# Fewer groups looked up ahead of the first step of a graph-convolution kernel, and two per step until the lead is reached

## The chip, the cores and the metric

One core of one Trainium2 chip runs the kernel as one launch. The metric is the device time in microseconds (us), median of the runs shown. PE is TensorE (PEld its weight loads), DVE is VectorE, ACT is ScalarE, POOL is GpSimd, SP is SyncE. "Span" is the time between first and last instruction of the profiled execution.

## The reference, cut to what matters

100,000 nodes with 128 features, 25,000 edges with a type out of 50, sorted by `dst`; `src` is random.

```python
h = maximum(layernorm(x), 0)                       # eps 1e-5
deg = segment_sum(ones, row)                       # row = src, col = dst
deg_inv = where(deg > 0, rsqrt(maximum(deg, 1)), 0)
norm = deg_inv[row] * deg_inv[col]
hj_b = comps[edge_type][:, :, None] * h[col][:, None, :]
msg = einsum('ebd,bdf->ef', hj_b, bases) * alpha[edge_type] * norm[:, None]
return x + segment_sum(msg, row)                   # 4 bases of 128 x 128
```

## The kernel before, in words

The 25,000 edges are 196 tiles of 128; four tiles are a group, so there are 49 groups. `x` is copied to the output by SP in 50 DMAs of 2,000 rows (`copy`, L295), at most two in flight. The edges' messages are then added onto the copy by indirect DMAs with an add, so POOL waits for all 50 copies before its first scatter (L365 to L367). Every engine has its own hand-written program, and semaphores alone tie them together. Within an engine, instructions run in the order written. The stages:

- **Histogram (degrees).** For each tile DVE writes one-hot rows of `src` (`hots`, L441 and L442) and PE multiplies them into four banks (L696), so that after 196 tiles the banks hold all degrees. After each 14 tiles comes a "type part": DVE's `type_hots(i)` (L434), PE's `turn_types(i)` (L688) and ACT's `keep_coef(i)` (L590). There are 14 parts; `turn_types(i)` waits until `keep_coef(i - 2)` has run, and DVE's `type_hots(i)` until `turn_types(i - 2)` has. POOL meanwhile gathers the rows `x[dst]` of 80 tiles (L356), and ACT takes their means and squares group by group (`stats(g)`, L575 to L583). ACT's program puts `keep_coef(i)` and the load of a later type row (`load_types`, L253) between the `stats`; `types_before(g)` says how many parts are kept before `stats(g)`.
- **Look-up.** To fetch the degrees of a tile's two ends, DVE writes one-hots of a whole group (`turned_hots(g)`, L458, four instructions, two buffers), PE multiplies them with the table of degrees (`look(t)`, eight matmuls at L710 into one of two banks), and DVE picks the value of each edge (`pick(t)`, two instructions at L464). `look(t)` waits for `pick(t - 2)`, `turned_hots(g)` for the looks of group g - 2, and the row of edges it reads is loaded by `load_edge_row(g)` (L260), which waits for `turned_hots(g - 4)`. Before, 8 groups (`LEAD`) are looked up ahead of step 0.
- **Norms.** For 7 groups at a time DVE computes degree products and variance (`norms_in`, L475 to L480), ACT a root (L595), DVE the coefficients (`norms_out`, L487 to L492).
- **49 steps**, one per group. PE turns the group's `h` (L720) and multiplies each tile by the four bases (`multiply(t)`, L729, waits for `message(t - 4)`); ACT takes the first base's part (`first(t)`, L620), DVE adds the three others (`combine`, L499), pair by pair of tiles. In the same step the group 8 ahead is looked up, one tile after each `multiply`. DVE also compares source ids within tiles (`same_src`, L518). From step 3 on, PE sums messages of equal source (`add_same`, L737 and L739), up to five tiles a step, ACT copies each sum into one of six buffers (`keep_sum`, L630), and POOL scatters it (L377). ACT runs `stats` of further groups at the end of a step: `stats_until(step)` is 21 + 2 (step + 1) groups, as far as gathered. POOL has gathered 112 tiles before its first scatter, and mixes the other 84 in, seven for ten scatters.

In ACT's program before the steps, five `load_edge_row` calls (groups 4 to 8) stand ahead of `stats(16)` to `stats(20)` (L639 to L642), and the last `keep_coef` calls stand behind some of them.

## Time and profile before

| what | value |
|---|---|
| median of 3 runs | 777.32 us (770.5 to 780.03) |
| the profiled execution | 778.24 us |
| its span | 776.5 us |
| mean granted TensorE clock | 0.919 |
| busy: PE, DVE, ACT, POOL | 74%, 77%, 47%, 69% |

The profiled execution lies 0.9 us above the median, and 1.7 us of it lie outside the span. Busy shares are means over stages with different limits, so the time is read stage by stage: the histogram until about 152 us, the look-ups until about 210 us, the steps until about 750 us, and the last scatters.

### The profile page before, as it was taken

Reading aid. Unit: us, or ns where it says so; the run is one execution under the profiler, and the core shown is the slowest. Engines: PE = TensorE matmul, PEld = TensorE weight load, DVE = VectorE, ACT = ScalarE, POOL = GpSimd, SP = SyncE. Lnnn points to the kernel's source line nnn. Section 1 sums busy time; section 2 is a strip of 40 time slices with the busy share of each in tenths; the row PEclk is TensorE's granted clock in tenths of the full one; section 3 lists DMA queues with packets and bytes.
Section 4 is the critical chain, followed back from the end, with each engine's and each line's share of the span. In section 5 each row is a group of like instructions: output and inputs, shape, how many; then the busy total and the mean of one; then the engine's idle time right before and its main releaser. Section 6 shows DMA issues by size and latency. Waiting matters only on the chain.

```text
span 776.5 us, 13645 instructions
## 1 busy us (share of the span) xinstructions
PE 575.3 (74%) x3922; PEld 408.1 (53%) x3922; DVE 596.3 (77%) x2613; ACT 368.7 (47%) x1493; POOL 538.5 (69%) x404
## 2 busy tenths in 40 slices
PE   1966795455776986687786977886898878898861
PEld 0744464444644754455554655654666656665530
DVE  4974795666777988677696979996989899998740
ACT  0155633153267554464455555565466634445630
POOL 1886687646500787877788887888888666667785
PEclk9996998778788999999899999998999999999995
DMA  3989999989811354444444545534444454534433
GB/s 114 341 308 339 338 351 314 354 283 337 308 33 55 73 95 76 82 93 78 96 78 87 93 63 117 94 56 94 93 93 84 82 93 81 100 58 55 59 34 28
DMA packets 56527, 108.89 MB, mean 140 GB/s; under 512 B 9291, under 2 KB 48216, under 8 KB 55636
## 3 DMA queue, kind: packets, MB, share of 16 engines
q0 software_dynamic: 34496, 25.72, 24.6%
q1 hardware_dynamic: 5372, 55.14, 19.6%
q10 hardware_dynamic: 16584, 27.16, 11.4%
q8 instruction: 32, 0.52, 0.3%
q14 instruction: 43, 0.35, 0.1%
HBM read 94.89 MB, written 64.61 MB: 205 GB/s over the span
## 4 chain that ended last, share of the span: by engine, by line
DVE 28%; PE 22%; DMA 14%; issue 12%; ACT 11%; POOL 8%; another core or an unknown queue 2%; SPq 1%; ACTq 0%; POOLq 0%; DVEq 0%
DMA out_dram<-acc,scatter_idx 9%; PE pst L710 7%; PE pst L696 6%; DVE masked L464 6%; POOL out_dram L377 5%; PE pst L729 5%; DVE part_sum L499 5%; DVE turned_hot L458 4%; DMA rows<-in_x_dram,dst_i 4%; POOL rows L356 3%; ACT scratch L583 3%; DVE rows L441 3%; ACT scratch L575 3%; DVE same L518 3%; DVE rows L499 2%
## 5 line engine op out<-in xcount | busy, mean ns | idle before, releaser
L377 POOL DMA_INDIRECT out_dram<-acc,scatter_idx x196 | 313.4, 1599 | 132.2 <-ACT acc L630 62.0
L356 POOL DMA_INDIRECT rows<-in_x_dram,dst_i x196 | 223.0, 1138 | 98.8 <-issue 40.9
L710 PE MATMUL pst<-table_bits,turned_hot 128*128 128x198 f16 x1568 | 181.4, 263 | 59.3 <-DVE masked L464 50.5
L729 PE MATMUL pst<-bases_sb,h_turned 128*128 128x512 f32 x392 | 212.6, 625 | 0.0
L710 PEld LDWEIGHTS pst<-table_bits,turned_hot 128*128 128x128 f16 x1568 | 145.9, 104 | 86.4 <-issue 52.8
L499 DVE SCALAR_TENSOR_TENSOR part_sum<-pst,coef,part_sum 128x128 f32<-128x128 f32 x392 | 115.8, 344 | 89.6 <-ACT part_sum L620 88.2
L737 PEld LDWEIGHTS pst<-rows,same 128*128 128x128 f32 x392 | 71.6, 197 | 177.7 <-issue 154.3
L464 DVE SCALAR_TENSOR_TENSOR masked<-iota_h,lo,pst 128x198 f32<-128x198 f16 x392 | 141.6, 415 | 16.9 <-PE pst L710 14.9
L620 ACT ACTIVATE part_sum<-pst,coef 128x128 f32<-128x128 f32 x196 | 71.2, 363 | 139.6 <-PE pst L729 102.9
L737 PE MATMUL pst<-rows,same 128*128 128x128 f32 x392 | 83.4, 296 | 66.1 <-ACT acc L630 62.1
L575 ACT ACTIVATE scratch<-rows 128x128 f32<-128x128 f32 x196 | 57.8, 297 | 135.8 <-DMA rows<-in_x_dram,dst_i 100.4
L696 PE MATMUL pst<-rows 128*128 128x198 f16 x784 | 94.3, 270 | 26.6 <-DVE rows L442 15.7
L630 ACT ACTIVATE acc<-pst,sum_scale 128x128 f32<-128x128 f32 x196 | 71.6, 365 | 77.2 <-DMA out_dram<-acc,scatter_idx 58.7
L441 DVE TENSOR_SCALAR rows<-iota_h,src_hi 128x512 f16<-128x512 f16 x196 | 68.7, 350 | 34.8 <-PE pst L696 19.0
L696 PEld LDWEIGHTS pst<-rows 128*128 128x128 f16 x784 | 67.0, 106 | 51.3 <-DVE rows L442 32.4
L518 DVE SCALAR_TENSOR_TENSOR same<-src_row,src_f,later 128x256 f32<-128x256 int32 x196 | 87.3, 478 | 0.0
L458 DVE TENSOR_SCALAR turned_hot<-edge_row,chunk_id 128x1024 f16<-128x1024 f16 x196 | 85.6, 499 | 0.0
L739 PE MATMUL pst<-acc,same 128*128 128x128 f32 x390 | 78.3, 284 | 0.0
L583 ACT ACTIVATE scratch<-rows,less_mean 128x128 f32<-128x128 f32 x196 | 76.2, 390 | 2.5 <-ACT less_mean L579 1.0
L729 PEld LDWEIGHTS pst<-bases_sb,h_turned 128*128 128x128 f32 x392 | 62.0, 199 | 0.1
L739 PEld LDWEIGHTS pst<-acc,same 128*128 128x128 f32 x390 | 62.0, 200 | 0.0
L604 ACT ACTIVATE h<-rows,less_mean 128x128 f32<-128x128 f32 x196 | 61.9, 390 | 0.0
(71 smaller groups left out, 414.5 us busy)
## 6 DMA issues: line engine op xcount, KB each, us to landing
out_dram<-in_x_dram SPq DMA_DIRECT2D x50, 1000.0 KB
src_row<-src_rows ACTq DMA_DIRECT2D x25, 512.0 KB
edge_row<-edge_rows ACTq DMA_DIRECT2D x45, 256.0 KB
rows<-in_x_dram,dst_i POOLq DMA_INDIRECT x196
out_dram<-acc,scatter_idx POOLq DMA_INDIRECT x196
rows<-edge_rows ACTq DMA_DIRECT2D x10, 175.0 KB
edge_row<-edge_rows SPq DMA_DIRECT2D x4, 256.0 KB
src_row<-src_rows SPq DMA_DIRECT2D x2, 512.0 KB
```

The lines of the kernel that those rows point to most:

```text
L356: pool.indirect_dma_start(row(t), None, x, bass.IndirectOffsetOnAxis(ap=dst_i[:, t:t + 1], axis=0)) \
L377: pool.indirect_dma_start(out, bass.IndirectOffsetOnAxis(ap=scatter_idx[:, t:t + 1], axis=0), acc[:, t % ACC_RING, :], None, compute_op=AL ...
L458: last = dve.tensor_scalar(turned_hot[:, g % 2, c, :], hi, chunk_id[:, c:c + 1], None, ALU.is_equal)
L464: last = dve.scalar_tensor_tensor(out=masked[:, 2 * (t % 2) + k, :], in0=iota_h[:, 0:LO], scalar=lo[:, k, t:t + 1], in1=pst[:, LOOK + t % ...
L499: dve.scalar_tensor_tensor(out=to, in0=pst[:, PRODUCT + t % 4, term * D:(term + 1) * D], scalar=coef[:, t, term:term + 1], in1=part_sum[:, ...
L518: dve.scalar_tensor_tensor(out=same[:, t % SAME_RING, 0:w], in0=src_row[:, b, j * P:j * P + w], scalar=src_f[:, t:t + 1], in1=later[:, 0:w ...
L583: last = act.activation(scratch[:, 1, j, :], row(t), ACT.Square, bias=less_mean[:, t:t + 1], accum_out=squares[:, t:t + 1])
L696: last = pe.matmul(pst[:, HIST + c, 0:LO], hots[:, b, c * P:(c + 1) * P], hots[:, b, CHUNKS * P:], start=(t == 0), stop=(t == TILES - 1))
L710: last = pe.matmul(pst[:, LOOK + t % 2, k * LO:(k + 1) * LO], turned_hot[:, g % 2, c, k * W + j * P:k * W + (j + 1) * P], table[:, c * LO: ...
L729: pe.matmul(pst[:, PRODUCT + t % 4, :], h_turned[:, g % 2, j, :], bases_sb[:].rearrange("d b f -> d (b f)"), start=True, stop=True).then_i ...
L737: last = pe.matmul(pst[:, SUMS, 0:D], same[:, t % SAME_RING, 0:P], row(t), start=True, stop=(t == 0))
L739: last = pe.matmul(pst[:, SUMS, 0:D], same[:, (t - 1) % SAME_RING, P:2 * P], acc[:, (t - 1) % ACC_RING, :], start=False, stop=True)
```

## The change

Three groups (`FIRST_LOOK`) instead of eight are looked up ahead of step 0. `look_until(step)` is min(49, step + 9, 3 + 2 (step + 1)): steps 0 to 4 look up two groups each (3 and 4, 5 and 6, and so on to 11 and 12), and from step 5 on one group each, 8 ahead, as before. In a step with two groups PE makes two looks after each `multiply`, and DVE picks four tiles after each pair. The norms come in batches that end at groups 3, 7, 14, 21 and so on. ACT makes 18 instead of 21 `stats` before the steps, keeps the type parts earlier among them (four for five `stats` instead of seven for ten), and loads the edge rows of groups 4 and on at the start of the steps, two for a step while two groups are looked up. POOL makes gathers 80 to 87 paced by the looks and 88 to 111 paced by the products of steps 0 to 2.

```diff
+    FIRST_LOOK = 3
+    NORM_AT = (0, 3, *range(NORM_GROUPS, GROUPS + 1, NORM_GROUPS))
...
+    def look_until(step):
+        return min(GROUPS, step + LEAD + 1, FIRST_LOOK + 2 * (step + 1))
+
+    def looks_at(step, j):
+        a, b = (GROUP * look_until(s) for s in (step - 1, step))
+        return list(range(a + (b - a) * j // GROUP, a + (b - a) * (j + 1) // GROUP))
...
-    HIST_GATHERS, FIRST_GATHERS = 80, 112
+    HIST_GATHERS, LOOK_GATHERS, FIRST_GATHERS = 80, 88, 112
...
-    STATS_BEFORE = 21
+    STATS_BEFORE = 18
 
     def types_before(g):
-        return min(TYPE_PARTS, max(0, (7 * g + 6) // 10))
+        return min(TYPE_PARTS, max(0, (4 * g + 3) // 5))
...
-                elif HIST_GATHERS <= t < FIRST_GATHERS:
-                    pool.wait_ge(look_ps, (t - HIST_GATHERS + 1) * LEAD * GROUP // (FIRST_GATHERS - HIST_GATHERS))
+                elif HIST_GATHERS <= t < LOOK_GATHERS:
+                    pool.wait_ge(look_ps, (t - HIST_GATHERS + 1) * FIRST_LOOK * GROUP // (LOOK_GATHERS - HIST_GATHERS))
+                elif LOOK_GATHERS <= t < FIRST_GATHERS:
+                    pool.wait_ge(product_ready, (t - LOOK_GATHERS) // 2 + 1)
...
             for k in range(GROUPS):
-                ahead = k + LEAD
                 for pair in range(0, GROUP, 2):
                     combine(range(k * GROUP + pair, k * GROUP + pair + 2))
-                    if ahead < GROUPS:
-                        for j in (pair, pair + 1):
-                            pick(ahead * GROUP + j)
+                    for j in (pair, pair + 1):
+                        for t in looks_at(k, j):
+                            pick(t)
+                            looked = t + 1
                     if pair == 0:
-                        if ahead + 1 < GROUPS:
-                            turned_hots(ahead + 1)
+                        while hots_done < min(GROUPS, looked // GROUP + 2, look_until(k) + 1):
+                            turned_hots(hots_done)
+                            hots_done += 1
...
-                after = STATS_BEFORE - 1 - g
-                if after < LEAD + 1 - EDGE_RING:
-                    load_edge_row(act, LEAD - after)
                 stats(g)
-            batch = 2
+            batch, edge, rooted = 2, EDGE_RING, 1
             root(0)
             relu(0)
...
             for k in range(GROUPS):
-                if k + LEAD + 1 < GROUPS:
-                    load_edge_row(act, k + LEAD + 1)
+                while edge < min(GROUPS, look_until(k) + 1):
+                    load_edge_row(act, edge)
+                    edge += 1
...
             pe.wait_ge(table_ready, CHUNKS)
-            for t in range(LEAD * GROUP):
+            for t in range(FIRST_LOOK * GROUP):
                 look(t)
```

The line numbers of the changed kernel are higher by 10 to 18; the operations are the same. In ACT's program at the end of the `stats` before the steps, the kernel before has (L590 is `keep_coef`, L260 `load_edge_row`, L575 to L583 `stats`; the first row here is the square of `stats(15)`):

```order
L583 ACTIVATE scratch,squares<-rows,less_mean 128x128 x4
L260 DMA edge_row<-edge_rows 128x2x512
L575 ACTIVATE scratch,row_sum<-rows 128x128 x4
L579 ACTIVATE less_mean<-row_sum 128x4
L583 ACTIVATE scratch,squares<-rows,less_mean 128x128 x4
L590 ACTIVATE coef_parts<-pst 128x168
L260 DMA edge_row<-edge_rows 128x2x512
L575 ACTIVATE scratch,row_sum<-rows 128x128 x4
L579 ACTIVATE less_mean<-row_sum 128x4
L583 ACTIVATE scratch,squares<-rows,less_mean 128x128 x4
L590 ACTIVATE coef_parts<-pst 128x168
L260 DMA edge_row<-edge_rows 128x2x512
L575 ACTIVATE scratch,row_sum<-rows 128x128 x4
L579 ACTIVATE less_mean<-row_sum 128x4
```

and the changed kernel, at the same place (L605 is `keep_coef`, L590 to L598 are `stats`; from `stats(15)` to the root):

```order
L598 ACTIVATE scratch,squares<-rows,less_mean 128x128 x4
L605 ACTIVATE coef_parts<-pst 128x168
L590 ACTIVATE scratch,row_sum<-rows 128x128 x4
L594 ACTIVATE less_mean<-row_sum 128x4
L598 ACTIVATE scratch,squares<-rows,less_mean 128x128 x4
L605 ACTIVATE coef_parts<-pst 128x168
L590 ACTIVATE scratch,row_sum<-rows 128x128 x4
L594 ACTIVATE less_mean<-row_sum 128x4
L598 ACTIVATE scratch,squares<-rows,less_mean 128x128 x4
L611 ACT_TABLE_LOAD
L611 ACTIVATE norm_root<-norm_in 128x12
```

No edge row is loaded among the `stats` any more, and the last `keep_coef` stands ahead of `stats(17)` instead of `stats(20)`.

On DVE, between the last look-ups ahead of the steps and the end of step 0, the kernel before has (L458 `turned_hots`, L464 `pick`, L499 `combine`, L518 `same_src`, L487 to L492 `norms_out`):

```order
L458 TENSOR_SCALAR turned_hot<-edge_row,chunk_id 128x1024 x4
L464 SCALAR_TENSOR_TENSOR masked,picked<-iota_h,lo,pst 128x198 x8
L487 TENSOR_TENSOR coef_sum<-coef_parts 128x112
L488 TENSOR_TENSOR coef_sum<-coef_sum,coef_parts 128x112
L490 RECIPROCAL norm<-norm_root 128x28
L491 TENSOR_TENSOR norm<-norm,has_degree 128x28
L492 TENSOR_TENSOR coef<-coef_sum,norm 128x112
L499 SCALAR_TENSOR_TENSOR part_sum<-pst,coef,part_sum 128x128 x4
L499 SCALAR_TENSOR_TENSOR rows<-pst,coef,part_sum 128x128 x2
L464 SCALAR_TENSOR_TENSOR masked,picked<-iota_h,lo,pst 128x198 x4
L458 TENSOR_SCALAR turned_hot<-edge_row,chunk_id 128x1024 x4
L518 SCALAR_TENSOR_TENSOR same,copies<-src_row,src_f,later 128x256
```

and the changed kernel (L470 `turned_hots`, L476 `pick`, L513 `combine`, L532 `same_src`, L488 to L493 `norms_in`, L501 to L506 `norms_out`):

```order
L476 SCALAR_TENSOR_TENSOR masked,picked<-iota_h,lo,pst 128x198 x8
L488 TENSOR_SCALAR variance<-squares 128x12
L493 TENSOR_TENSOR norm_in<-norm_in,variance 128x12
L501 TENSOR_TENSOR coef_sum<-coef_parts 128x48
L506 TENSOR_TENSOR coef<-coef_sum,norm 128x48
L513 SCALAR_TENSOR_TENSOR part_sum<-pst,coef,part_sum 128x128 x4
L513 SCALAR_TENSOR_TENSOR rows<-pst,coef,part_sum 128x128 x2
L476 SCALAR_TENSOR_TENSOR masked,picked<-iota_h,lo,pst 128x198 x8
L470 TENSOR_SCALAR turned_hot<-edge_row,chunk_id 128x1024 x8
L532 SCALAR_TENSOR_TENSOR same,copies<-src_row,src_f,later 128x256
L513 SCALAR_TENSOR_TENSOR part_sum<-pst,coef,part_sum 128x128 x4
L476 SCALAR_TENSOR_TENSOR masked,picked<-iota_h,lo,pst 128x198 x8
```

`norms_in` now stands straight ahead of `norms_out`, with no `turned_hots` and no picks between them, and a step has eight picks' instructions and two groups' one-hots where it had four and one.

On PE the first two tiles of step 0 read before (L720 turns `h`, L729 is `multiply`, L710 `look`):

```order
L720 MATMUL pst<-ident,h 128x128 x8
L729 MATMUL pst<-bases_sb,h_turned 128x512
L710 MATMUL pst<-table_bits,turned_hot 128x198 x8
L729 MATMUL pst<-bases_sb,h_turned 128x512
L710 MATMUL pst<-table_bits,turned_hot 128x198 x8
```

and now (L733 `turn`, L742 `multiply`, L723 `look`):

```order
L733 MATMUL pst<-ident,h 128x128 x8
L742 MATMUL pst<-bases_sb,h_turned 128x512
L723 MATMUL pst<-table_bits,turned_hot 128x198 x16
L742 MATMUL pst<-bases_sb,h_turned 128x512
L723 MATMUL pst<-table_bits,turned_hot 128x198 x16
```

Each `multiply` has 16 matmuls of look-ups behind it instead of 8.

## Rows read from the trace of the kernel before

**Rows 1.** Stretches of 25 us: length, busy us (instructions) by engine, PE clock, DMA share, GB/s

```profile
core 0: us, PE busy (x) PEld busy (x) DVE busy (x) ACT busy (x) POOL busy (x), PEclk, DMA share, GB/s
...
450.00:475.00 25.00, 19.40 (x122) 13.87 (x121) 20.50 (x92) 11.74 (x44) 19.58 (x15) 0.93 0.46 79
...
650.00:675.00 25.00, 22.72 (x157) 16.68 (x156) 23.71 (x105) 12.00 (x36) 17.14 (x11) 1.00 0.42 70
```

**Rows 2.** The same over 2 us after the copies (same columns)

```profile
217.00:219.00 2.00, 2.00 (x18) 1.43 (x16) 2.00 (x7) 0.55 (x3) 0.00 (x0) 1.00 0.00 0
```

**Rows 3.** Timeline of POOL: start, us, engine, line, what; [idle before it, and its releaser]

```profile
253.32 1.63 POOL L377 DMA_INDIRECT out_dram<-acc,scatter_idx  x1 [42.63 <-ACT acc L630]
...
284.07 1.56 POOL L377 DMA_INDIRECT out_dram<-acc,scatter_idx  x1 [0.30 <-issue]
```

**Rows 4.** Timeline of PE in the histogram, at a type part (L688); columns as in rows 3

```profile
127.11 0.52 PE L688 MATMUL pst<-comps_split,rows 50*128 50x12 bf16 x14 [5.48 <-ACT coef_parts L590]
```

**Rows 5.** Timeline of ACT: keep_coef (L590) after stats(0), and the wait at an edge row load

```profile
34.14 0.29 ACT L590 ACTIVATE coef_parts<-pst 128x168 f32<-128x168 f32 x1
...
156.32 0.31 ACT L575 ACTIVATE scratch<-rows 128x128 f32<-128x128 f32 x1 [16.94 <-DVE turned_hot L458]
```

**Rows 6.** Groups by line, 20 to 54 us: busy us, mean ns | idle before, releasers

```profile
L356 POOL DMA_INDIRECT rows<-in_x_dram,dst_i x18 | 28.8, 1601 | 10.1 <-PE pst L696 9.2 <-issue 0.9
L441 DVE TENSOR_SCALAR rows<-iota_h,src_hi 128x512 f16<-128x512 f16 x70 | 24.2, 346 | 0.0
```

**Rows 7.** Groups by line, 160 to 210 us (the look-ups)

```profile
L356 POOL DMA_INDIRECT rows<-in_x_dram,dst_i x32 | 31.8, 994 | 24.1 <-PE pst L710 15.6 <-issue 7.3 <-remote 1.1
...
L688 PE MATMUL pst<-comps_split,rows 50*128 50x12 bf16 x14 | 0.5, 169 | 8.0 <-ACT coef_parts L590 8.0
```

**Rows 8.** Timeline of all engines: first look, then the changeover to the steps

```profile
160.31 7.19 PE L710 MATMUL pst<-table_bits,turned_hot 128*128 128x198 f16 x48
...
203.23 0.18 DVE L475 TENSOR_SCALAR variance<-squares 128x28 f32<-128x28 f32 x1
...
204.45 2.43 ACT L604 ACTIVATE h<-rows,less_mean 128x128 f32<-128x128 f32 x8
...
209.50 0.42 DVE L464 SCALAR_TENSOR_TENSOR masked<-iota_h,lo,pst 128x198 f32<-128x198 f16 x1 [0.55 <-PE pst L710]
...
211.50 1.02 PE L729 MATMUL pst<-bases_sb,h_turned 128*128 128x512 f32 x2
...
214.14 0.37 ACT L620 ACTIVATE part_sum<-pst,coef 128x128 f32<-128x128 f32 x1 [0.66 <-PE pst L729]
```

**Rows 9.** Groups by line, 211 to 300 us: what a step is made of

```profile
L710 PE MATMUL pst<-table_bits,turned_hot 128*128 128x198 f16 x232 | 28.2, 270 | 9.5 <-DVE masked L464 9.2 <-issue 0.2
...
L464 DVE SCALAR_TENSOR_TENSOR masked<-iota_h,lo,pst 128x198 f32<-128x198 f16 x56 | 20.1, 416 | 0.0
L499 DVE SCALAR_TENSOR_TENSOR part_sum<-pst,coef,part_sum 128x128 f32<-128x128 f32 x56 | 16.7, 345 | 15.9 <-ACT part_sum L620 15.9
...
L458 DVE TENSOR_SCALAR turned_hot<-edge_row,chunk_id 128x1024 f16<-128x1024 f16 x28 | 11.8, 486 | 0.0
```

**Rows 10.** Timeline of ACT in step 2 and at the start of step 3

```profile
237.87 0.34 ACT L620 ACTIVATE part_sum<-pst,coef 128x128 f32<-128x128 f32 x1
...
244.38 0.37 ACT L620 ACTIVATE part_sum<-pst,coef 128x128 f32<-128x128 f32 x1 [4.01 <-PE pst L729]
...
250.83 0.35 ACT L620 ACTIVATE part_sum<-pst,coef 128x128 f32<-128x128 f32 x1
251.08 0.35 ACT L630 ACTIVATE acc<-pst,sum_scale 128x128 f32<-128x128 f32 x1
```

**Rows 11.** The chain that ended last, in order of time (start, us, what)

```profile
65.42 4.65 another core or an unknown queue
```

**Rows 12.** Timeline: ACT issues the load of type row 4; DVE uses it

```profile
32.62 0.56 ACTq L253 DMA_DIRECT2D rows<-edge_rows  x1
...
50.88 0.68 DVE L434 TENSOR_SCALAR rows<-rows,chunk_id 50x1792 bf16<-50x1792 f16 x1
```

75 lines of the change are left out of this document (39 added, 36 removed).

## The prediction

> **What bounds the kernel now.** I read the stretches of 25 us first, then POOL's timeline, then PE's and ACT's timelines of the histogram and of the changeover to the steps. In the stretch from 450 us POOL is busy 19.58 of 25 us with 15 instructions, and each has 0.30 us of issue ahead of it: 24.1 of 25 us [rows 1, 3]. So POOL's scatters and gathers set the pace of the middle of the kernel. Late in the kernel, when the gathers are done, DVE is the fuller engine (from 650 us 23.71 of 25 us, POOL 17.14 with 11 scatters) [rows 1]. The first scatter starts at 253.32 us, after POOL has idled 42.63 us for ACT's first sum [rows 3]. The copies that it must also wait for are over by 217 us, when DMA traffic is zero [rows 2]. So the end of the kernel follows the first scatter: whatever brings it forward comes through to the end, as long as POOL stays fed afterwards. At most 36 us can be won there (253.3 to about 217).
>
> What lies ahead of the first scatter is a chain of four pieces: the histogram up to the first look at 160.31 us, the look-ups up to the first `multiply` at 211.50 us, and steps 0 to 2 with the start of step 3 up to the scatter, 41.8 us [rows 3, 8]. The change touches every piece.
>
> **First look (removed waits).** PE could not begin to look at 160.31 us sooner because its last type part waited 8.0 us for a `keep_coef` [rows 7], and ACT, which makes it, stood 16.94 us at the load of edge row 4, until DVE's first one-hots were written [rows 5]. The edge rows leave this place, so this wait goes. That alone lets looks start when the one-hots are there, at 156.3 at the latest: 4 us.
>
> The earlier `keep_coef` calls do more. Within the histogram PE waits for them too, 5.48 us at one part [rows 4], because they stand behind `stats` that wait for gathers. The last part on which PE waits needs `keep_coef(11)`, and that now stands behind `stats(14)` instead of `stats(16)`. So the look-ups can start when 15 groups are gathered and treated. `stats(0)` is done at 34.14 us [rows 5]. While DVE writes one-hots without a pause a gather takes 1.60 us plus 0.30 us of issue, 7.6 us for a group [rows 3, 6], and 14 more groups end at 34.1 + 14 x 7.6 = 140.7 us. At the pace of the look-up stage (0.99 + 0.30, 5.2 us a group [rows 7]) they end at 107 us, and then the histogram is its own limit: 70 tiles in 34 us are 0.49 us a tile [rows 6], so 196 tiles from just before 20 us end by about 113 us and looks start at some 117 us. Against this stand pauses in which nothing that the trace names is waited for, the longest of them 4.65 us [rows 11]; I see no reason for them to go. Bounds: 117 and 156.3 us. I take 138 us, near the slow pace, a little less because PE still has pauses in which gathers run quickly. That is 22 us earlier than now (bounds 4 and 43).
>
> On that pace the Trainium skill (SBUF — State Buffer, section "SBUF: two separate sides") says that a VectorE instruction in a two-port mode locks GpSimd out for its whole length, so that indirect DMAs issued there wait to have their descriptors written. The two means, 1.60 us beside the one-hots and 0.99 us beside the look-ups, agree with it. By this rule a histogram with fewer pauses gathers more slowly, which speaks against the change: its own limit would be 140.7 us, and without the rule 117 us.
>
> **Look-ups and changeover.** Eight groups take 160.31 to 209.50 us, 6.15 us a group; three take 18.4 us. Before, the norms (begun at 203.23 us) and ACT's eight ReLU instructions (204.45 us, 2.43 us long) ran beside the look-ups of group 7, and `multiply(0)` came 2.0 us after the last pick's start [rows 8]. Now nothing covers them. After the last look: two picks 0.8 us, norms and root 1.2 us (203.23 to 204.45), ReLUs 2.4 us, ACT's copy of the turned group and the semaphores 0.9 us: 5.3 us. So `multiply(0)` follows the first look by 23.7 us instead of 51.2 us, a gain of 27 us (bounds 24 and 29, by 3 us more or 2 us less of exposed work). `multiply(0)` would start at 162 us.
>
> **Steps 0 to 2 (added work).** In step 2 ACT goes from `first(8)` at 237.87 to `first(11)` at 244.38 (6.5 us), does two `stats` (6.45 us) and starts `first(12)` at 250.83: 12.96 us a step [rows 10]. The first 6.5 us are a chain through the engines, and the second group's look-ups lie right in it. By busy time over count in [rows 9], a `combine` of a pair is 6 x 0.298 = 1.8 us, a pick 2 x 0.359 = 0.72 us, a look 8 x 0.122 = 0.97 us, one group's one-hots 4 x 0.42 = 1.7 us. From `first(b)`, 0.75 us into the step: `combine` 1.8; then PE's third and fourth look, each waiting for a pick, with DVE's picks 3.4; the one-hots of the second group, which PE has not had before, 1.7; two looks 1.9; `multiply` 1.1; semaphores 0.9. Sum 11.6 us to `first(d)`. With `stats` 6.45 us and the return to `first` that makes 18.2 us instead of 12.96 us: 5.3 us more a step. The picks and one-hots behind `first(d)` fit beside the two `stats`. Step 0 has one look more ahead of its second product (1 us), and the four-group norms between steps 1 and 2 hold ACT's root by about a microsecond. Together 3 x 5.3 + 2, and 2 for uneven starts: 20 us. Bounds: 9 us (one look more a tile hidden, 3 us a step) and 35 us (10 us of work for each further group wholly in line with DVE's present step). The first scatter then comes at 162 + 41.8 + 20 = 224 us, behind the end of the copies, so the floor of 217 us does not act.
>
> **Steps 3 and 4 (POOL fed more slowly).** Before, the eleventh scatter starts 30.75 us after the first [rows 3], with POOL never idle. The eleventh sum is made in step 5. Two double steps of 18.2 us, with three `add_same` in the chain of each, put it about 40 us after the first (an `add_same` is four matmuls in the records, and at a look's 0.122 us each [rows 9] about 0.5 us: 36.4 + 6 x 0.5 = 39.4 us). POOL waits for the difference, 9 us (bounds 0 and 17). From step 5 on the program is the same as before, and POOL, which is the limit there, cannot make it up. This is what I would expect a reader to overlook: the first scatter gains 29 us, the end only 20.
>
> **Sum.** 22 + 27 - 20 - 9 = 20 us. From the profiled 778.2 us that is 758 us; the profiled execution lies 0.9 us above the median, which changes nothing at this accuracy. So the five groups that leave the lead-in are paid back nearly whole in the double steps (27 against 29), and what stays is the earlier start of the look-ups.
>
> **Rivals.**
> - *The histogram does not shorten.* The looks then start at 156.3 us, 4 us earlier, and the other terms give 4 + 27 - 29 = 2: 776 us. For it: the unnamed pauses, and the slow gathers, which a denser histogram makes slower. Against it: PE's measured waits for `keep_coef` [rows 4, 7].
> - *The double steps hide their looks.* DVE idles 15.9 us at `combine` between 211 and 300 us [rows 9]. If that takes up half of the work, the steps cost 10 us and POOL stays fed: 22 + 27 - 10 = 39, cut by the end of the copies to 36: 742 us.
> - *Edge rows land late, and it is slower.* Two edge rows a step are now issued just ahead of the step that uses them, some 8 us before DVE needs the first, while the copies still fill the DMA engines (steps 0 to 2 lie between 162 and 217 us). The nearest row is a type row issued at 32.62 us and used at 50.88 us without a wait [rows 12], so a broadcast under the copies takes at most 18 us. If it takes all of that, each of three steps waits 10 us more: 20 - 30 = -10, 788 us. It decides once the wait exceeds 6 to 7 us a step. Against it: the 18 us are only an upper bound, since the row may have lain there long before it was used.
>
> **How the numbers follow.** The forecast has a chance of 0.5, with a range of its own from 748 to 768 us; the unshortened histogram 0.2; the hidden looks 0.2; the late edge rows 0.07; anything else 0.03. Two per cent, about what a measurement of this kernel can tell from no change, is 762 us and 793 us. Of the forecast's half, 0.33 lies below 762 us. With the hidden looks that is 0.53 for faster; 0.43 for within two per cent, with the first and most of the third rival; 0.04 for slower. The range from 740 to 780 us leaves out the late edge rows and the ends of the others.
>
> **What would show it.** Right: PE's first look near 138 us with no `keep_coef` wait of 8 us ahead of it; `multiply(0)` about 24 us later; steps 0 to 4 of some 18 us each with DVE waiting for `first(d)`; the first scatter near 224 us; POOL idle between scatters 6 and 11 and without gaps after them. Wrong: a first look later than 150 us, double steps under 15 us, a first scatter held by the last copy, or waits of DVE's one-hots for `edge_row`.

## The result: slower by one per cent, where 2.6% faster was forecast

| | us |
|---|---|
| this kernel, median of 12 runs | 780.93 (773.57 to 785.49) |
| kernel before, median of 12 runs on the same chip | 773.75 (768.83 to 783.61) |
| ratio, 95% interval | 1.0099 (1.0063 to 1.0134) |
| predicted | 758.0, range 740 to 780 |

By the 2% bound this is no change; by its interval it is a small, real loss. The profiled execution took 785.49 us (span 783.6), 4.6 us above its median; it is the slowest of the twelve and counts as a slow run, which the ratio leaves out, while e13 below profiles the same kernel in a fast run. Differences of a few microseconds between two profiles are left to the ratios.

**Profile after.** Its page begins as follows; the 40 slices are 19.6 us each.

```profile
span 783.6 us, 13659 instructions
...
PE 583.6 (74%) x3922; PEld 414.5 (53%) x3922; DVE 597.8 (76%) x2624; ACT 371.0 (47%) x1494; POOL 538.4 (69%) x404
...
PEclk9996898967888889999899999998999999999995
```

No engine gained or lost noticeable work, so the loss is waiting. The two stretches that answer to [rows 1] (same columns) still show POOL as the fuller part of the middle, and DVE late:

```profile
450.00:475.00 25.00, 20.77 (x129) 14.88 (x129) 20.78 (x94) 11.97 (x43) 20.73 (x15) 0.93 0.50 105
650.00:675.00 25.00, 21.95 (x152) 16.29 (x151) 23.79 (x109) 10.92 (x31) 16.19 (x11) 1.00 0.49 81
```

Milestones of the two profiled executions, read from the timelines of PE and POOL, beside what was forecast:

| start of, us | before | forecast | after | after less before |
|---|---|---|---|---|
| first look | 160.31 | 138 | 145.58 | -14.7 |
| `multiply(0)` | 211.50 | 162 | 173.46 | -38.0 |
| first scatter | 253.32 | 224 | 242.02 | -11.3 |
| eleventh scatter | 284.07 | 264 | 286.82 | +2.8 |
| last scatter | 768.6 | | 775.7 | +7.1 |

The lead-in did shorten by 38 us. All of it is gone again by the eleventh scatter. POOL's timeline after (columns as in [rows 3]) shows the second half of the loss:

```profile
242.02 1.63 POOL L389 DMA_INDIRECT out_dram<-acc,scatter_idx  x1 [8.72 <-issue]
...
257.02 1.78 POOL L389 DMA_INDIRECT out_dram<-acc,scatter_idx  x1 [2.82 <-ACT acc L646]
263.65 1.57 POOL L389 DMA_INDIRECT out_dram<-acc,scatter_idx  x1 [3.53 <-ACT acc L646]
...
272.02 1.60 POOL L389 DMA_INDIRECT out_dram<-acc,scatter_idx  x1 [3.59 <-ACT acc L646]
...
286.82 1.56 POOL L389 DMA_INDIRECT out_dram<-acc,scatter_idx  x1 [5.10 <-ACT acc L646]
290.00 1.81 POOL L389 DMA_INDIRECT out_dram<-acc,scatter_idx  x1 [0.30 <-issue]
```

Before, POOL had 0.30 us of issue ahead of the eleventh scatter [rows 3]; now it waits for ACT's sum again and again up to it, and behind it about as rarely as before. From the first to the eleventh scatter it is 44.8 us instead of 30.75 us (46.9 us in e13).

The first half is in steps 0 to 2, which start at 173.46, 195.19 and 217.36 us, with step 3 at 237.40 us: 21.7, 22.2 and 20.0 us each, where 18.2 us was forecast and 12.96 us was the step of before [rows 10]. The chain that ended last runs through them. Here is a part of it (start, us, what) from the end of step 0 to step 4:

```profile
189.65 1.17 ACT scratch L590 x8
...
194.16 0.43 ACT scratch L598 x2
194.60 13.96 DMA edge_row<-edge_rows
209.07 1.72 DVE turned_hot L470 x4
210.79 0.81 DVE same L532 x4
211.60 1.04 DVE part_sum L513 x4
212.63 0.52 DVE rows L513 x2
213.15 0.69 DVE masked L476 x4
213.89 2.82 PE pst L723 x16
216.71 0.85 PE pst L733 x4
217.56 1.63 PE pst L742 x2
...
233.93 2.82 PE pst L723 x16
236.75 0.85 PE pst L733 x4
237.60 1.71 PE pst L742 x2
...
256.21 1.17 ACT scratch L590 x8
257.64 1.65 ACT scratch L598 x8
259.29 1.18 ACT scratch L590 x8
260.73 0.79 ACT scratch L598 x3
```

Three things are to be read here. The load of an edge row stood in ACT's program behind the two `stats` of step 0, took 13.96 us to land, and DVE's one-hots (L470) waited 3.56 us for it. From there to `multiply(12)`, at the start of step 3, the chain goes through one-hots, `combine` (L513), picks (L476), looks (L723), `turn` (L733) and `multiply` (L742), and ACT is not in it. From step 3 on ACT's `stats` (L590, L598) stand in it themselves.

ACT's and PE's timelines over the end of step 2 say the same from the side of the wait:

```profile
230.64 0.37 ACT L636 ACTIVATE part_sum<-pst,coef 128x128 f32<-128x128 f32 x1 [3.77 <-PE pst L742]
...
239.40 0.37 ACT L636 ACTIVATE part_sum<-pst,coef 128x128 f32<-128x128 f32 x1 [2.23 <-issue]
```

```profile
228.15 1.56 PE L723 MATMUL pst<-table_bits,turned_hot 128*128 128x198 f16 x16 [1.69 <-DVE turned_hot L470]
...
233.93 2.82 PE L723 MATMUL pst<-table_bits,turned_hot 128*128 128x198 f16 x16 [3.33 <-DVE masked L476]
```

From `first(11)` to `first(12)` it is 8.76 us, where it was 6.45 us for the two `stats` before [rows 10]; the same way in steps 0 and 1 takes 7.11 and 11.18 us, where it was 6.44 us before. In step 2 ACT finishes them and then idles 2.23 us, because `multiply(12)` stands on PE behind the last looks of step 2. Those looks are also slow. After an idle of 3.33 us sixteen of their matmuls take 2.82 us instead of 1.56 us, and the granted clock of that stretch is 0.50, the 1.2 GHz level (stretches of 2 us, columns as in [rows 1]):

```profile
228.00:230.00 2.00, 1.85 (x17) 1.62 (x18) 1.97 (x7) 0.00 (x0) 1.49 (x2) 1.00 0.11 33
234.00:236.00 2.00, 2.00 (x13) 1.83 (x14) 1.08 (x7) 1.94 (x13) 0.00 (x0) 0.50 0.11 33
```

### The profile page after: what moved, and what is told of

It is laid out like the page before. It is cut to its first block, busy times and chain, and to the rows that moved or that the text cites. A ratio compares the mean times of both kernels' runs of the same rounds, so it can differ in the third digit from the quotient of the medians.

```text
span 783.6 us, 13659 instructions
## 1 busy us (share of the span) xinstructions
PE 583.6 (74%) x3922; PEld 414.5 (53%) x3922; DVE 597.8 (76%) x2624; ACT 371.0 (47%) x1494; POOL 538.4 (69%) x404
## 3 DMA queue, kind: packets, MB, share of 16 engines
q10 hardware_dynamic: 16584, 27.16, 11.6%
## 4 chain that ended last, share of the span: by engine, by line
DVE 24%; PE 19%; issue 17%; DMA 16%; POOL 15%; ACT 7%; another core or an unknown queue 1%; SPq 1%; ACTq 0%; POOLq 0%; DVEq 0%
DMA out_dram<-acc,scatter_idx 12%; POOL out_dram L389 10%; PE pst L723 6%; PE pst L709 5%; POOL rows L368 5%; DVE masked L476 4%; PE pst L742 4%; DVE turned_hot L470 4%; DVE rows L453 4%; DVE part_sum L513 3%; DVE rows L454 3%; ACT scratch L598 2%; DMA edge_row<-edge_rows 2%; DVE rows L513 2%; DVE same L532 2%
## 5 line engine op out<-in xcount | busy, mean ns | idle before, releaser
L723 PE MATMUL pst<-table_bits,turned_hot 128*128 128x198 f16 x1568 | 181.5, 265 | 80.9 <-DVE masked L476 61.6
L742 PE MATMUL pst<-bases_sb,h_turned 128*128 128x512 f32 x392 | 218.1, 640 | 0.0
L723 PEld LDWEIGHTS pst<-table_bits,turned_hot 128*128 128x128 f16 x1568 | 147.2, 105 | 108.3 <-issue 52.5
L513 DVE SCALAR_TENSOR_TENSOR part_sum<-pst,coef,part_sum 128x128 f32<-128x128 f32 x392 | 115.8, 344 | 98.6 <-ACT part_sum L636 92.3
L750 PEld LDWEIGHTS pst<-rows,same 128*128 128x128 f32 x392 | 74.4, 203 | 168.1 <-issue 147.2
L476 DVE SCALAR_TENSOR_TENSOR masked<-iota_h,lo,pst 128x198 f32<-128x198 f16 x392 | 141.8, 416 | 18.9 <-PE pst L723 11.6
L590 ACT ACTIVATE scratch<-rows 128x128 f32<-128x128 f32 x196 | 57.7, 297 | 94.0 <-DMA rows<-in_x_dram,dst_i 87.4
L453 DVE TENSOR_SCALAR rows<-iota_h,src_hi 128x512 f16<-128x512 f16 x196 | 68.4, 349 | 26.8 <-PE pst L709 15.5
L470 DVE TENSOR_SCALAR turned_hot<-edge_row,chunk_id 128x1024 f16<-128x1024 f16 x196 | 85.5, 500 | 3.6 <-DMA edge_row<-edge_rows 3.6
L532 DVE SCALAR_TENSOR_TENSOR same<-src_row,src_f,later 128x256 f32<-128x256 int32 x196 | 87.3, 478 | 0.4 <-issue 0.4
L752 PE MATMUL pst<-acc,same 128*128 128x128 f32 x390 | 79.9, 289 | 0.0
L598 ACT ACTIVATE scratch<-rows,less_mean 128x128 f32<-128x128 f32 x196 | 76.2, 390 | 2.0 <-ACT less_mean L594 0.5
L752 PEld LDWEIGHTS pst<-acc,same 128*128 128x128 f32 x390 | 63.7, 205 | 0.0
L742 PEld LDWEIGHTS pst<-bases_sb,h_turned 128*128 128x128 f32 x392 | 63.5, 204 | 0.2
```

The lines of the kernel that those rows point to most:

```text
L453: dve.tensor_scalar(hots[:, b, 0:CHUNKS * P], iota_h[:], src_hi[:, t:t + 1], None, ALU.is_equal)
L470: last = dve.tensor_scalar(turned_hot[:, g % 2, c, :], hi, chunk_id[:, c:c + 1], None, ALU.is_equal)
L476: last = dve.scalar_tensor_tensor(out=masked[:, 2 * (t % 2) + k, :], in0=iota_h[:, 0:LO], scalar=lo[:, k, t:t + 1], in1=pst[:, LOOK + t % ...
L513: dve.scalar_tensor_tensor(out=to, in0=pst[:, PRODUCT + t % 4, term * D:(term + 1) * D], scalar=coef[:, t, term:term + 1], in1=part_sum[:, ...
L532: dve.scalar_tensor_tensor(out=same[:, t % SAME_RING, 0:w], in0=src_row[:, b, j * P:j * P + w], scalar=src_f[:, t:t + 1], in1=later[:, 0:w ...
L723: last = pe.matmul(pst[:, LOOK + t % 2, k * LO:(k + 1) * LO], turned_hot[:, g % 2, c, k * W + j * P:k * W + (j + 1) * P], table[:, c * LO: ...
```

## The experiments

Every ratio is against the kernel before on the same chip. No run has a profile of the kernel before on the second group's chips; e10, which has its lead-in, stands in for it there. The changed kernel and e1 to e8 ran on chips on which it takes 774 to 775 us, the others on chips on which it takes 754 to 755 us, so only ratios are compared between the two groups, never times. "Milestones" are first look, `multiply(0)`, first scatter, eleventh scatter, from one profiled execution each.

### What the earlier type parts bring: e1 and e2

e1 is the kernel before with the new times of the `keep_coef` calls alone; e2 is the changed kernel with the old times and 21 groups of `stats` ahead of the steps.

```diff
# e1, on before
-        return min(TYPE_PARTS, max(0, (7 * g + 6) // 10))
+        return min(TYPE_PARTS, max(0, (4 * g + 3) // 5))
# e2, on after
-    STATS_BEFORE = 18
+    STATS_BEFORE = 21
-        return min(TYPE_PARTS, max(0, (4 * g + 3) // 5))
+        return min(TYPE_PARTS, max(0, (7 * g + 6) // 10))
```

> The kernel before with one thing of the change alone: keep_coef four parts for five stats (types_before) instead of seven for ten; eight groups are still looked up ahead of step 0, and the edge rows are still loaded among the stats. Theory 1 (in the change the histogram part gained and the double steps gave it back): the first look starts at about 145 us as in the changed kernel (145.58) instead of 160.31, everything behind it moves by the same amount, the first scatter comes at about 239 us, the time is 13 to 16 us shorter than before: ratio 0.980 to 0.984. Rival A (the earlier keep_coef is not what brought the first look forward, it was the removal of the edge rows from among the stats): the first look stays later than 155 us, ratio 0.995 to 1.00. Rival B (an earlier first scatter is lost again behind it, because something other than POOL's scatters sets the end): first look at 145 us, but ratio above 0.99.

> The changed kernel with the histogram part undone: keep_coef again seven parts for ten stats, 21 stats ahead of the steps; still no edge row loads among them, three groups ahead of step 0 and two a step. Theory 1: the first look goes back to about 156 us (10 us later than in the changed kernel), but steps 0 to 4 have three stats fewer between them, worth 3 x 3.2 us mostly in steps 3 and 4; time 0 to 8 us longer than the changed kernel, ratio to the kernel before 1.01 to 1.02. Rival A (the edge rows were what held the first look): first look stays near 146 us and the time falls by the stats saved, ratio to before about 1.00.

Measured: e1 0.998 (0.9945 to 1.0014), milestones 138.14, 204.17, 248.1, 277.47. e2 1.0034 (1.0004 to 1.0064), milestones 153.41, 177.27, 244.46, 282.54.

In e1 the first look comes 22 us earlier, just what the prediction's first term said, and yet `multiply(0)` only 7.3 us earlier: the look-ups now take 66.0 us instead of 51.2 us. DVE's waits (us in total, times, longest) give one reason, before and in e1:

```profile
DVE rows L441 <- remote: 15.5, 5, 4.7
```

```profile
DVE masked L464 <- remote: 18.1, 4, 10.6
```

"Remote" are the pauses of [rows 11], in which nothing that the trace names is waited for. Before, they fell into the histogram (L441); in e1 most of them fell into the look-ups (L464). But they are not the whole reason. e12 and e10, below, ran on a chip without such pauses and differ ahead of the steps by the early type parts alone: the first look comes 11.7 us earlier (130.69 instead of 142.38 us), and `multiply(0)` only 2.8 us (182.63 instead of 185.41 us). In e12's look-ups ACT waits 20.7 us for gathered rows (e10: 5.8 us) ahead of its `stats`, and the loads of the edge rows stand in its program behind them:

```profile
DVE turned_hot L460 <- DMA edge_row<-edge_rows: 6.3, 3, 3.7
```

So on that chip the look-ups that start earlier wait for edge rows, and these for the gathers (the row is from 130 to 183 us). e2 changes two things at once and does not price the early type parts: without them and with three more groups of `stats` ahead of the steps, the changed kernel is no worse, rather 0.65% better (intervals that just touch).

### What slows the double steps: e4, e3, e11, e8

```diff
# e4, on after (e8: the same on before, with the types of e1)
-        return min(STATS_BEFORE + 2 * (step + 1), ...)
+        return min(STATS_BEFORE + (step + 1), ...)
# e3, on after: edge rows 4 to 7 ahead of root(0); at the end of step k, ahead of the stats
+                while edge < min(GROUPS, look_until(k + 2) + 1):
+                    load_edge_row(act, edge)
+                    edge += 1
# e11, on after, ahead of the looks of j = 1 and 3 in steps 0 to 4; u = 4k + j + 1
+                        pe.wait_ge(message_ready, u - 3)
+                        for _ in range(10):
+                            pe.matmul(pst[:, PRODUCT + u % 4, 0:LO], iota_h[:, 0:P], iota_h[:, 0:LO],
+                                      start=True, stop=True)
```

The matmuls added in e11 keep PE busy and are never read.

> The changed kernel with one stats call at the end of a step instead of two (the total is the same, spread over more steps, in which ACT has room). Theory 1 (ACT's two stats stand in line with the doubled look-up chain): each of steps 0 to 4 gets 3.2 us shorter, the first scatter comes some 9 us earlier (233 us), POOL is fed 6 us better in steps 3 and 4, time 10 to 15 us shorter than the changed kernel, ratio to before 0.99 to 0.995. Rival D (the stats are beside DVE's picks of the second pair, so DVE's work takes their place): steps shorten by less than 1.5 us each, time within 5 us of the changed kernel.

> The changed kernel with each edge row loaded one step earlier: rows 4 to 7 ahead of ACT's first root, then the two of step k + 2 at the end of step k. Rival C (late edge rows make the double steps slow): DVE's wait for an edge row (3.56 us once, after a load that took 13.96 us to land) goes, the first scatter comes 4 us or more earlier than the 242.0 us of the changed kernel, and the time is 4 to 10 us shorter than the changed kernel's (ratio to before 0.995 to 1.004). Theory 1 (the looks, picks and one-hots in line are what cost): steps 0 to 4 still take 18 to 21 us each, the time is 0 to 4 us shorter.

> The changed kernel with ten extra matmuls (128x198, f16, result never read) on PE ahead of the second and fourth pair of looks in each of steps 0 to 4, where PE idles 2.6 us now and then runs the looks at half clock (16 matmuls in 2.82 us instead of 1.56). Theory 3 (the lower clock after these idles is what makes a double step 22 us instead of the 18 forecast): the looks behind them take 1.56 us, the way from the first multiply to the first scatter falls from 68.6 us by 5 us or more, time 5 to 8 us shorter than the changed kernel. Theory 1 without the clock: the way gets no shorter, or longer by up to 1.3 us per group of extra matmuls, time the same or up to 5 us longer.

> The kernel before (eight groups looked up ahead, single steps) with the early keep_coef and with one stats call per step instead of two. Theory 1 (two stats stand in line in every early step, also in single ones): steps 0 to 3 take 10 us instead of 13, the first scatter comes 7 to 9 us earlier than with the early keep_coef alone, time 764 to 768 us, ratio to before 0.985 to 0.991, shorter than both kernels. Rival: POOL is as late with one stats call because gathers then wait for stats: no gain over the early keep_coef alone (0.998).

| | ratio (95%) | `multiply(0)` to first scatter | first to eleventh |
|---|---|---|---|
| before | 1 | 41.8 | 30.75 |
| after | 1.0099 (1.0063 to 1.0134) | 68.6 | 44.8 |
| e4 | 0.9954 (0.9919 to 0.999) | 64.3 | 38.1 |
| e3 | 1.0076 (1.0038 to 1.0114) | 64.3 | 45.6 |
| e11 (after there: 69.5, 46.9) | 1.007 (1.0038 to 1.0102) | 69.3 | 42.7 |
| e8 | 0.9966 (0.9924 to 1.0007) | 37.3 | 30.15 |

One `stats` fewer per step is the largest single piece: 1.4% against the changed kernel, 11 us on the way to the eleventh scatter, of which 6.7 us lie behind the first scatter and only 4.3 us in steps 0 to 2. That fits the chain above, in which `stats` stand from step 3 on. Up to the eleventh scatter POOL's scatters wait 9.8 us for ACT's sums in e4, and 17.0 us in the changed kernel. In steps 0 to 2 of e4 the way from `first(d)`, the last `first` of a step, to the next step's first one still takes 9.97, 7.85 and 7.89 us, though one `stats` is only 3.2 us, and ACT idles 6.52, 4.40 and 4.44 us at its end:

```profile
196.22 0.37 ACT L636 ACTIVATE part_sum<-pst,coef 128x128 f32<-128x128 f32 x1 [6.52 <-PE pst L742]
```

So in these steps it is the work on DVE and PE behind `first(d)` that is waited for, not the `stats`.

The early edge rows (e3) take away the wait for the load (no such row in DVE's waits) and 4.3 us of steps 0 to 2, but the time only moves within its uncertainty (its profile is of its fastest run, 771.61 us; the median is 780.15 us). In e11 most looks of the double steps run at the 2.4 GHz level, and two groups of sixteen, behind longer idles, still do not:

```profile
170.39 2.82 PE L723 MATMUL pst<-table_bits,turned_hot 128*128 128x198 f16 x16 [6.03 <-DVE masked L476]
...
180.83 1.56 PE L723 MATMUL pst<-table_bits,turned_hot 128*128 128x198 f16 x16 [1.71 <-DVE masked L476]
```

The mean granted clock between `multiply(0)` and the first scatter is 0.91 instead of 0.75 in e13, and the way is as long as there, 69.3 us against 69.5 us. The time gains 0.3 to 0.5% against the changed kernel, with overlapping intervals. So the half clock is not shown to cost anything here; what the added matmuls themselves cost is not known apart. e8 shows the same cut of `stats` on the kernel before: the steps get shorter by 6.7 us against e1, and 3.3 us are left at the eleventh scatter. That would be 0.4% of the time, and the ratio moves by 0.14%, which its interval cannot tell from either.

### The copies, and the pauses: e5, e6, e7

e5 (on before) and e6 (on after) leave out 48 of the 50 copies from the input to the output, so most output rows lack their input part. e7 is the changed kernel with 100 copies of half the size.

```diff
# e5, e6
-            for i in range(1, COPIES):
-                copy(i)
+            copy(1)
-                sp.wait_ge(copied[b], 16 * (COPIES // COPY_RING))
+                sp.wait_ge(copied[b], 16)
# e7
-    COPIES = 50
+    COPIES = 100
```

> The kernel before, leaving out 48 of the 50 copies of x to the output (rows 4,000 and up are not copied), so that the lead-in has the DMA engines nearly to itself. If the copies are behind the unnamed pauses and the slow gathers: no pause of the unnamed kind is left, the first look comes at 115 to 130 us, the first multiply some 45 to 50 us later, the first scatter at 205 to 215 us, time 730 to 740 us. If the pauses are not due to the copies: they stay, and the first look is later than 140 us.

> The changed kernel with the same 48 copies left out. Theory 1 (the chain of doubled looks, and POOL fed late in steps 3 and 4, give back what the shorter look-up won, whatever the DMA load): the eleventh scatter comes within 5 us of that of the kernel before without copies, and the two times lie within 6 us of each other. Rival (theory 2: the change loses because its double steps 0 to 2 now lie under the copies, with late edge rows and pauses): without copies the changed kernel is at least 10 us shorter than the kernel before without copies, with double steps of 15 us or less.

> The changed kernel with 100 copies of 1,000 rows instead of 50 of 2,000, still two in flight, so that half as much stands queued in the DMA engines ahead of a gather, an edge row or an instruction fetch. Theory 2 (the queue of the copies is what delays the lead-in and steps 0 to 2): gathers land in about 5 us instead of 7.5, the edge row load that took 13.96 us takes less than 9, the pauses halve, time 8 to 15 us shorter than the changed kernel (ratio to before 0.990 to 0.998). If only the total of bytes counts: no change beyond 0.3%. If the copies get slower by the smaller size, they end after 230 us and the first scatter waits for them: longer than the changed kernel.

Measured: e5 1.0021 (0.9968 to 1.0073), e6 1.0088 (1.0045 to 1.0132), e7 1.0591 (1.0539 to 1.0644). Taking the DMA load away changes no time by more than its uncertainty, in either kernel, and the eleventh scatters of e5 and e6 lie at 281.4 and 282.2 us, so the loss does not need the copies. Steps 0 to 2 alone do get shorter, though: 60.4 us lead from `multiply(0)` to the first scatter of e6, with no wait for an edge row, where the forecast was 61.8 us and the changed kernel has 68.6 us; 45.5 us then follow to the eleventh. The pauses stay, and the gathers remain as slow beside DVE's one-hots as in [rows 6] and as quick beside the look-ups as in [rows 7]. DVE's waits, then POOL's gathers from 20 to 54 us and from 160 to 210 us, all of e5:

```profile
DVE rows L440 <- remote: 27.8, 7, 6.6
```

```profile
L355 POOL DMA_INDIRECT rows<-in_x_dram,dst_i x19 | 29.7, 1562 | 10.4 <-PE pst L695 9.2 <-issue 1.2
...
L355 POOL DMA_INDIRECT rows<-in_x_dram,dst_i x32 | 32.1, 1003 | 25.2 <-PE pst L709 17.6 <-issue 7.6
```

So the copies are not why gathers take 1.6 us; what the trace has left beside them is DVE's one-hots, as the prediction assumed; no run took those away. In e7 the copies themselves became slower: all traffic between 175 and 200 us is 244 GB/s, where the kernel before has 339 GB/s. They end near 290 us instead of 217 us, and the first scatter waits for them, 63.63 us long:

```profile
250.00:275.00 25.00, 11.50 (x59) 8.10 (x56) 10.75 (x46) 7.77 (x39) 0.00 (x0) 0.64 0.80 245
...
291.65 1.63 POOL L389 DMA_INDIRECT out_dram<-acc,scatter_idx  x1 [63.63 <-issue]
```

So the end of the copies is a floor for the first scatter, and in e7 nothing else decides when it comes.

### The changed kernel on a chip without pauses: e13

> The changed kernel, unchanged, on the same chip as the next three. If the pauses without a named cause are part of why it is slower: on a chip without them the ratio is 1.000 or less. If the double steps alone are the cause: ratio 1.006 to 1.014 again, with the first multiply 35 to 42 us earlier than in the kernel before, the way from it to the first scatter 60 us or more, and the eleventh scatter 38 us or more after the first, whether or not pauses are seen.

Measured: 765.01 us against 755.35 us, 1.0118 (1.0059 to 1.0177). Its profile has no pause of this kind, and both kernels are 16 to 18 us shorter than on the first chip. The loss is the same, so the pauses are not its cause. `multiply(0)` comes at 154.06 us, 31.4 us earlier than in e10 (185.41 us) and not the 35 to 42 us expected; the steps take 24.0, 20.3, 21.6 and 20.2 us, 69.5 us lead to the first scatter and 46.9 us from there to the eleventh. DVE's one-hots wait for an edge row three times, 5.2 us in all, behind loads that ACT issues at the start of steps 0 and 2 and that land up to 17 us later.

### Sums that start a step earlier: e9, e10, e12, e14, e16

```diff
# e9 on after, e10 on before
-    SUM_STEP, SUM_RATE = 3, 5
+    SUM_STEP, SUM_RATE = 2, 5
# and in same_until
+        if step < 0:
+            return 0
```

e12 is e10 with the types of e1 and one `stats` a step. e14 is the changed kernel with the edits of e3, e4, e9 and e11 together. e16 is e10 with `FIRST_GATHERS` 128 instead of 112.

> The changed kernel with the sums, and so the scatters, starting in step 2 instead of step 3 (SUM_STEP 2; the comparisons of source ids move up by a step with them). Theory 1 (the time follows the eleventh scatter, and POOL is fed late while the double steps last): the first scatter comes at the end of step 2, near 232 us instead of 242.0, since it must wait for product 12 anyway; the eleventh comes some 15 us earlier than the changed kernel's 286.8; time 10 to 15 us shorter than the changed kernel, ratio to before 0.990 to 0.997. Rival (the double steps get longer by the sums put into step 2, and POOL's start does not matter): eleventh scatter within 5 us of 286.8, time as the changed kernel.

> The kernel before with the sums starting in step 2. POOL is already never idle after its first scatter there. Theory 1: the first scatter comes at about 242 us instead of 253.3, the eleventh 31 us after it, time 8 to 12 us shorter than before, ratio 0.984 to 0.990. Rival: sums one step earlier only pile up, the later steps being bound by DVE: ratio 0.997 or more.

> The kernel before with three things: the early keep_coef, one stats call per step, the sums from step 2 on. If the eleventh scatter sets the time, the gains add: first scatter at about 235 us, eleventh at about 266 us, time 758 to 763 us, ratio to before 0.978 to 0.985. If one of them covers the other: ratio 0.988 or more.

> The changed kernel with edge rows a step earlier, one stats call per step, extra matmuls in PE's idles, and sums from step 2 on. Theory 1 (the looks, picks and one-hots in line remain): double steps still 15 us or longer, eleventh scatter no earlier than that of the kernel before with sums from step 2 (249.1 us on the pause-free chip), ratio to before 0.985 to 0.995, no better than the 0.9892 of the kernel before with that one edit. Rival (the surroundings were the cost): double steps of 13 us, ratio 0.98 or less.

> The kernel before with sums from step 2 on and 128 instead of 112 tiles gathered ahead of the first scatter, while POOL is idle. The end follows POOL's work behind its first scatter until the gathers are done: 16 gathers of 1.3 us less there, up to 21 us; some of it is lost because DVE takes over as the limit earlier. Expect ratio to before 0.972 to 0.982. Rival (DVE is the limit already): ratio as with sums from step 2 alone, 0.989.

| | ratio (95%) | first scatter | eleventh |
|---|---|---|---|
| e9 | 1.0003 (0.9958 to 1.0048) | 217.19 | 254.65 |
| e10 | 0.9892 (0.9856 to 0.9927) | 219.13 | 249.11 |
| e12 | 0.9919 (0.9884 to 0.9954) | 221.35 | 251.64 |
| e14 | 0.9901 (0.9862 to 0.9939) | 222.22 | 251.75 |
| e16 | 0.9865 (0.9814 to 0.9917) | 222.13 | 251.16 |

The earlier start of the sums is worth 1% in both kernels. Alone, on the kernel before, it beats both kernels of this study. With it the first scatter is at the floor in all five: ACT's first sum starts at 201.16 us in e9, 211.76 us in e10, 205.42 us in e12, 194.12 us in e14 and 213.43 us in e16. In e12 ACT's first sum is done by 205.8 us, DMA traffic ends by 218 us, and POOL starts at 221.35 us. The first sum, two stretches and the scatter:

```profile
205.42 0.35 ACT L632 ACTIVATE acc<-pst,sum_scale 128x128 f32<-128x128 f32 x1
```

```profile
216.00:218.00 2.00, 2.00 (x21) 1.92 (x20) 1.93 (x12) 0.90 (x3) 0.00 (x0) 1.00 0.01 4
218.00:220.00 2.00, 1.54 (x9) 0.87 (x6) 2.00 (x10) 1.94 (x12) 0.00 (x0) 1.00 0.00 0
```

```profile
221.35 1.63 POOL L379 DMA_INDIRECT out_dram<-acc,scatter_idx  x1 [27.04 <-issue]
```

That is why e12, with all that e8 had, is no better than e10, and why e14, the changed kernel with the edits of e3, e4 and e11 together, is no better than e10 either: its first sum is ready 28 us before its first scatter. e14's steps 0 and 1 still take 18.1 and 16.7 us: with one `stats` and early loads, and no wait for an edge row, the chain of two groups' picks, one-hots and looks is what is left of them. Its steps 2 and 3 (18.9 and 23.8 us) say nothing on that, because there ACT waits for a free sum buffer while POOL cannot scatter yet (from 192 to 236 us):

```profile
ACT acc L648 <- DMA out_dram<-acc,scatter_idx: 14.6, 4, 8.2
```

e16 is the fastest of all, though its interval overlaps e10's. Its last gather comes 60 us earlier (504.6 instead of 565.1 us), and yet the eleventh and the last scatter lie 487.0 us apart, as in e10 (487.4 us). So 16 gathers fewer for POOL did not shorten this way; what sets it is open, and that it is DVE, as expected, is not shown.

### Five groups ahead instead of three: e15

```diff
-    FIRST_LOOK = 3
+    FIRST_LOOK = 5
+            while edge < FIRST_LOOK + 1:
+                load_edge_row(act, edge)
+                edge += 1
```

> The changed kernel with FIRST_LOOK 5: five groups ahead of step 0 and double steps only 0 to 2 (edge rows 4 and 5 loaded ahead of ACT's first root). Theory 1 (a group looked up in a double step costs about 8 us, in the lead-in 6.2 us): the ratio lies between that of the changed kernel and 1, at 1.000 to 1.006. If the loss is not in the number of double steps but in what comes with any of them (fewer stats ahead, edge rows late): ratio as the changed kernel's, within 0.2 per cent.

Measured: 1.0191 (1.0138 to 1.0245), milestones 129.88, 177.53, 241.68, 272.55. A middle way is worse than either end, but for a reason of its own: the two edge rows more land late, for 14.5 us of waiting inside the look-ups. DVE's waits in the whole program:

```profile
DVE turned_hot L470 <- DMA edge_row<-edge_rows: 17.2, 3, 9.3
```

With the loads issued early enough this number could come out otherwise; that was not tried. But e15 isolates another term: with double steps 0 to 2 only, steps 3 and 4 are single again, and from the first to the eleventh scatter it is 30.87 us, as before (30.75 us), where e13 on the same chip has 46.9 us. So the slow feeding of POOL comes from the double steps 3 and 4.

## Why the prediction was wrong, step by step

Forecast and result lie 27 us apart in the profiles: 20 us of gain against 7.1 us of loss. By the prediction's own terms:

- **The end follows the scatters: right.** From the eleventh scatter to the start of the last it is 484 to 489 us in all kernels of the first group, whatever came ahead (before 484.5, e1 484.8, e4 489.1, e7 486.4, after 488.9), and 485 to 488 us in the second, except for e9 (494.8). The difference of 4.4 us between before and after lies within that spread and is no cause. Why the way has this length is another matter: the prediction has POOL as the limit, and e16 does not bear that out.
- **First look, forecast +22: too large.** It came 14.7 us earlier. The reasoning on `keep_coef` held (e1 reached 138.14 us, the forecast was 138 us). e3 and e4, which share the changed kernel's lead-in, have their first look at 144.67 and 138.49 us, so single executions differ by 7 us here, and the size of this miss is uncertain. What failed was "I see no reason for them to go" as the only word on the pauses: they neither went nor stayed in the histogram, some moved into the look-ups. (The bound 34.1 + 14 x 7.6 is 140.5, not 140.7, which changes nothing.)
- **Look-ups and changeover, forecast +27: nearly right.** The first look was followed by `multiply(0)` after 27.9 us instead of 51.2 us: +23.3 us. Two pauses of 4.3 and 1.7 us in the look-ups are more than the difference to the forecast's 23.7 us. Both terms together gave 38 of 49 us: 11 us missing.
- **Steps 0 to 2, forecast -20: the mis-sized term.** They cost 26.7 us. The sentence that failed is "The picks and one-hots behind `first(d)` fit beside the two `stats`". The way from `first(a)` to `first(d)` was sized nearly right: 13.8, 11.7 and 11.4 us in steps 0 to 2, forecast 11.6 us (the forecast's sum begins with the 0.75 us from the start of the step). But the return from `first(d)` to the next step, which the sum left at 6.45 us, took 7.11, 11.18 and 8.76 us, 7.7 us more in all (5.6 us in e13), because on PE the next step's `multiply` is queued behind looks that wait for picks that wait for the last `combine`. e4 shows that it is not the `stats`: with one of them gone the return still takes 7.9 to 10 us. That those looks run at half clock is in the chain too (2.82 us instead of 1.56 us), but e11, at a higher clock, has as long a way. Into step 1 came the late edge row, with 3.56 us: the third rival's mechanism, though not three waits of 10 us.
- **Steps 3 and 4, forecast -9: same sign, too small.** 14 us. Here the two `stats` do stand in the chain, e4 gives back 6.7 us of it, and e15, with single steps 3 and 4, all of it. The forecast took 18.2 us for each double step and about 0.5 us for each `add_same`; measured from `first(12)` to `first(20)` the two steps take 46.1 us. (Before, POOL was not quite "never idle": one of its scatters waited 1.53 us for an earlier one.)
- **Sum.** 11 us missing ahead of the steps, 6.7 and 5 us more in them, and 4.4 us of spread behind make the 27 us. The central idea, that the five groups are paid back in the steps, was right and understated: 38.0 us won, 40.8 us paid by the eleventh scatter.
- **Rivals.** The late edge rows (788 us) came closest to the profiled 785.5 us, in time only: they waited 3.56 us (5.2 us in e13) where the rival has 30 us, and e3, without such a wait, is still 0.8% slower than before. The unshortened histogram (776 us) has the wrong sign. The hidden looks (742 us) fell: DVE's wait for `first` in the whole program rose from 88.2 to 92.3 us instead of being filled.

e4 and e3 measured their terms singly, and e11 found none for the clock; that the remainder of a double step (17 to 18 us) is the chain of picks, one-hots and looks itself rests on steps 0 and 1 of e14 and on the chain rows, and no run took this chain out. Of the 1% loss, one `stats` too many per double step is alone large enough to explain it: without it (e4) the kernel is 0.5% faster than before, while the same cut on the kernel before (e8 against e1) brings nothing that could be measured.

## What to carry to other kernels

Work moved out of a lead-in into the steps is free only if it does not stand on an engine's queue between two links of the step's own chain; read who is queued behind the last moved instruction (here the next `multiply`) and not only how idle the engines are. A head start is worth what is left of it where the queue that the rest of the kernel follows, here POOL's scatters, is first fed without a gap. Where that queue simply starts late, starting it a step earlier (e10, one constant, 1.1%) beats shortening all that stands ahead of it.

## What the runs showed of the hardware that was not expected

- **Pauses without a name.** On the first group's chips DVE stood 15.5 us in all for nothing that the trace names (before) and 27.8 us in e5, with DMA traffic nearly gone, so the copies are not their cause. In the profiles taken on the two chips of the other group there is not one. They stand in the rows of DVE, ACT and POOL. In e1 one of them lasted 10.63 us on DVE, and no packet of the instruction queues fell into it. Their cause is open.
- **Smaller copies were slower.** With 500 KB instead of 1000 KB a copy, two in flight as before, the traffic between 175 and 200 us was 244 instead of 339 GB/s (before). The Trainium skill (DMA: Bandwidth & Descriptors, section "Bandwidth") advises transfers of at least 1 MiB, beside a table for loads from HBM into SBUF; the run, with copies from one DRAM tensor to another, agrees in direction. It cost 4.9% against the changed kernel because the first scatter waits for the last copy.
- **Half clock in short idles.** PE fell to the 1.2 GHz level in the double steps, for instance in looks that follow idles of 3.33 and 5.88 us. Raising the mean granted clock from 0.75 to 0.91 (e11 against e13) left the way to the first scatter as it was, 69.3 against 69.5 us: the looks were faster, and nothing was gained by it.
